# Two attention stages: TensorE issues scores and exponents in pairs and value products two units at a time; VectorE's work between the maxima is put in another order

## What is computed

```python
# first kind, causal (stage a0)
q_rot, k_rot = rotate(q), rotate(k)
scores = einsum('bhqd,bhkd->bhqk', q_rot, k_rot) / sqrt(dh) + decay_bias
scores = where(causal, scores, -inf)
x = x + (softmax(scores) @ v) @ Wo.T
...
# second kind, no mask (stage a1)
q, k, v = layernorm per head of (x @ Wq + bq), (x @ Wk + bk), (x @ Wv + bv)
scores = einsum('bqhd,bkhd->bhqk', q, k) * scale
x = x + (softmax(scores) @ v) @ Wo + bo
```

## Time and profile before

| | |
|---|---|
| median of 3 runs | 2072.04 us (2063.23 to 2077.58) |
| profiled execution | 2082.38 us, its span 2080.5 us |
| TensorE busy | 1543.0 us (74%) |
| VectorE busy | 1178.1 us (57%) |
| ScalarE busy | 720.2 us (35%) |
| GpSimd busy | 940.2 us (45%) |
| `a0` in its steady steps | 410 to 744 us of the span, 11 batches |
| `a1` in its steady steps | 1400 to 1757 us of the span, 10 batches |

### The profile page before, as it was taken

One profiled execution on the slowest core, in us unless ns is written; L12 is line 12 of the kernel. 1 busy time (PEld: TensorE's weight loads), 2 busy tenths in 40 slices (PEclk: granted clock), 3 DMA queues, 4 the chain that ended last, 5 costly groups with the idle time before them and its releaser, 6 DMA issues. The chain is left out here.

```text
span 2080.5 us, 34781 instructions
## 1 busy us (share of the span) xinstructions
PE 1543.0 (74%) x10592; PEld 938.6 (45%) x10592; DVE 1178.1 (57%) x4262; ACT 720.2 (35%) x1339; POOL 940.2 (45%) x1276
## 2 busy tenths in 40 slices
PE   1329938999999998399233992598878788993990
PEld 1219923444444444299222881233333333433880
DVE  3622245566666664122594554777778778843555
ACT  1102213455555553022001330354445445631330
POOL 2745524233443432155474773634454536422771
PEclk9999965999999999599555995587888879965995
DMA  6152210000000000522223882000000000004884
GB/s 219 44 117 66 72 45 16 6 22 16 15 20 10 11 11 13 105 72 69 75 73 97 245 240 67 12 6 16 16 15 14 16 5 11 12 11 106 238 238 130
DMA packets 93868, 134.91 MB, mean 65 GB/s; under 512 B 14784, under 2 KB 72512, under 8 KB 93760
## 3 DMA queue, kind: packets, MB, share of 16 engines
q1 hardware_dynamic: 62768, 88.27, 15.5%
q0 software_dynamic: 17408, 35.82, 5.1%
q10 hardware_dynamic: 13584, 9.48, 1.9%
HBM read 80.61 MB, written 52.91 MB: 64 GB/s over the span
## 5 line engine op out<-in xcount | busy, mean ns | idle before, releaser
L1345 ACT ACTIVATE a_PT<-a_psE 128x512 f32<-128x512 f32 (+1 forms) x512 | 278.0, 543 | 446.0 <-PE a_psE L1509 444.5
L1054 DVE TENSOR_REDUCE a_mx<-a_psS 128x2 f32<-128x512 f32 (+1 forms) x512 | 312.5, 619 | 145.3 <-PE a_psS L1475 144.5
L1532 PE MATMUL a_psV<-a_PT,a_vx 128*32 128x256 f32 (+1 forms) x2048 | 321.8, 397 | 3.0 <-ACT a_PT L1345 0.6
L1475 PE MATMUL a_psS<-a_KT,a_QT 54*128 54x256 bf16 (+1 forms) x1024 | 196.4, 282 | 66.8 <-DVE a_mx L1054 65.5
L1509 PE MATMUL a_psE<-a_QM,a_KT 56*128 56x256 bf16 (+1 forms) x1024 | 199.8, 278 | 1.6 <-issue 0.8
L1907 POOL DMA_INDIRECT slots_y<-e_y,e_ids x160 | 155.3, 970 | 46.6 <-issue 24.4
L1837 PE MATMUL e_psH<-e_rowsT,e_w 128*128 128x256 f32 x640 | 160.3, 395 | 6.4 <-DMA e_w<-in_pack 4.7
L1475 PEld LDWEIGHTS a_psS<-a_KT,a_QT 54*128 54x128 bf16 x1024 | 56.7, 96 | 200.7 <-DVE a_mx L1054 103.5
L1754 POOL DMA_INDIRECT slots_y<-e_y,e_ids x128 | 124.2, 971 | 48.7 <-POOL e_ids L1752 29.2
L1532 PEld LDWEIGHTS a_psV<-a_PT,a_vx 128*32 128x32 f32 x2048 | 77.0, 112 | 118.2 <-issue 82.8
L1837 PEld LDWEIGHTS e_psH<-e_rowsT,e_w 128*128 128x128 f32 x640 | 118.7, 196 | 25.0 <-issue 6.0
(11 more groups left out here) (329 smaller groups left out, 3117.1 us busy)
## 6 DMA issues: line engine op xcount, KB each, us to landing
e_w<-in_pack SPq DMA_DIRECT2D x80, 450.0 KB
e_rows<-slots_x SPq DMA_DIRECT2D x80, 129.0 KB, 2.6
e_rows<-spans_x SPq DMA_DIRECT2D x64, 129.0 KB
a_got<-slots_y SPq DMA_DIRECT2D x32, 256.0 KB
t_got<-slots_y SPq DMA_DIRECT2D x32, 256.0 KB
slots_y<-e_y,e_ids POOLq DMA_INDIRECT x288, 2.2
spans_x<-tail ACTq DMA_DIRECT2D x8, 516.0 KB, 13.4
spans_x<-tail SPq DMA_DIRECT2D x8, 516.0 KB, 17.1
```

The source lines that it names most:

```text
L1054: nc.vector.tensor_reduce(mx[u][:, t, 4 * g + r:4 * g + r + 3:2], psS[c % 2][:, :, 0:cols], AX, ALU.max).then_inc(s_max, 1)
L1345: nc.scalar.activation(PT[:, c % 4, :, q0:SEQ], psE[c % 2][:, :, q0:SEQ], ACT.Exp).then_inc(s_e, 1)
L1475: last = nc.tensor.matmul(psS[c % 2][:, hh, 0:cols], QT[u][64 * r:64 * r + MAXR, k, t * P:(t + 1) * P], KT[u][64 * r:64 * r + MAXR, k, 0:c ...
L1532: last = nc.tensor.matmul(psV[g // 2][32 * quad:32 * quad + 32, g % 2, q0:SEQ], vx[u][:, kt, head, :], PT[:, c % 4, hh, q0:SEQ], start=(kt ...
```

## The change

On TensorE, `unit_scores` and `unit_e` are cut into an opening (waits and, in `a0`, the mask) and single heads. Scores `n+2` and exponents `n+1` are now issued together: both openings, then the heads in turn. `unit_c` gives `r` from `c % 2`, so that the two units of such a pair always lie in different halves of the array. Value products are issued for two units at once, at every even `n`, and the two units now have different `r` and the same tile of keys, so that the four heads lie in four different column strips.

```diff
@@ unit_c @@
-            return c // 4, (c // 2) % 2, c % 2
+            return c // 4, c % 2, (c // 2) % 2
@@ TensorE, step @@
                 if has(s):
-                    unit_scores(s, u, 0)
-                    unit_scores(s, u, 1)
+                    for c in range(2):
+                        scores_open(s, c)
+                    for hh in range(2):
+                        for c in range(2):
+                            scores(u, c, hh)
                 if has(s - 3):
                     routed_tiles(s - 3, v)
+                if has(s - 1):
+                    e_open(s - 1, 0)
+                    for hh in range(2):
+                        e(v, 0, hh)
                 for n in range(UNITS):
-                    if has(s - 1):
-                        unit_e(s - 1, v, n)
-                        if n >= 1:
-                            unit_v(s - 1, v, n - 1)
+
+                    if has(s) and n < UNITS - 2:
+                        scores_open(s, n + 2)
+                    if has(s - 1) and n < UNITS - 1:
+                        e_open(s - 1, n + 1)
+                    for hh in range(2):
+                        if has(s) and n < UNITS - 2:
+                            scores(u, n + 2, hh)
+                        if has(s - 1) and n < UNITS - 1:
+                            e(v, n + 1, hh)
+
+                    if has(s - 1) and n >= 2 and n % 2 == 0:
+                        unit_v(s - 1, v, n - 2)
+                        unit_v(s - 1, v, n - 1)
                     if n == 0 and has(s - 2):
                         back(s - 2, u, 0)
...
-                    if has(s) and n < 14:
-                        unit_scores(s, u, n + 2)
-                if has(s - 1):
-                    unit_v(s - 1, v, 15)
                 if has(s + 1):
                     operands(s + 1, v, 3)
+                if has(s - 1):
+                    unit_v(s - 1, v, UNITS - 2)
+                    unit_v(s - 1, v, UNITS - 1)
```

```diff
@@ Combine @@
+    def dve_add_one(self, dve, link, b, u, w, k, t):
+        link.sync()
+        if k == 0 and t == 0:
+            wait(dve, self.s_got[w], (b - w) * (16 // self.held) + 16)
+        ins = nc.vector.scalar_tensor_tensor(
...
+        if k == TOPK - 1 and t == TPB - 1:
+            link(ins)
+            nc.vector.tensor_copy(self.used[:, u:u + 1], self.gate[:, u, 0:1]).then_inc(self.s_added, 1)
+        else:
+            link.later(ins)
...
@@ VectorE, step @@
-                if has(s - 1):
-                    queries_out(s - 1)
...
                 maxima(0, 1)
-                if has(s + 3) and not causal:
-                    comb.dve_add(dve, link, s + 3, v)
+                if has(s + 3):
+                    comb.dve_gate(dve, link, s + 3, v)
+                add(0, 0)
                 maxima(1, 2)
...
                 if has(s):
                     max_rows(s, u)
+                if has(s + 1):
+                    last_operand_out(s + 1, v)
+                if has(s):
+                    queries_out(s)
+                if has(s - 1):
+                    weighted_out(s - 1, v)
                 if has(s + 3):
                     norm.dve_apply(dve, s + 3, v)
-                if has(s - 1):
-                    weighted_out(s - 1, v)
-                if has(s + 1):
-                    last_operand_out(s + 1, v)
```

89 lines of the change are left out of this document (47 added, 42 removed).

## The result

The changed kernel takes 1991.12 us (median of 4 runs, 1962.49 to 2008.29); the kernel before, beside it on the same chip, 2069.68 us (2063.23 to 2077.58). The ratio is 0.957, with a 95% interval of 0.949 to 0.964. (Disturbed runs are left out of the ratio, which is why it is not the quotient of the medians.) The profiled execution took 1987.22 us with a span of 1985.4. It is faster by 4%; the forecast was 6%.

The account below looks back on a forecast made before the run. TensorE was taken to bound `a0`, waits to decide `a1`. Gains of 88 us in `a0`, 41 in `a1`, 5 at stage ends, less 6 in token stages, took 128 off: profiled 1954, median 1944, range 1888 to 1995.

Parts of the forecast that it names:

- the four strips: TensorE's value products: four heads in four column strips take one unit's time, saving 3.6 us a batch.
- 31.1 at full clock: Batch of `a1`: VectorE's work, gaps and waits at full clock sum to 31.1 us, from 35.7 before.
- hence 32.8: Batch of `a1` with 1.7 us added for TensorE's doubtful clock: 32.8 us, from 30.0 to 35.7.
- Logits, "no wait": VectorE in `a1`: reading the logits later removes their wait, 2.8 us a batch before.
- Projections, "0.9 is left. The second: none": VectorE in `a1`: first projection's wait shrinks to 0.9 us a batch, second's to none; 4.0 us together before.
- The batch's end, 1.4: VectorE waits 1.4 us at each batch's end for operands and queries TensorE transposes last, in `a0` and `a1`.
- Scores met late, 0.9: VectorE in `a1` waits 0.9 us a batch for scores met late.
- The clock, +1.7 for 0.83 and more: TensorE's clock in `a1`, 0.83 before: slow stretches lengthen waits by 0 to 4.5 us a batch, taken as 1.7.
- Additions, "I take VectorE's work as unchanged": VectorE in `a1`: spreading the four additions leaves GpSimd's blocks, so its work stays unchanged.
- The queries first: VectorE's batch end: operand and queries copies directly follow `max_rows`, normalisation and `weighted_out` come behind; 1.4 us of waits.
- Token stages, -6: VectorE in `t1` and `t2`: additions each wait for the one before, losing 4 to 7 us, taken as 6.
- the wait is replaced in `a1`: Rival: low TensorE clock returns the readers' gain at batch's end and projection; `a1` stays 35.7, total 1985 us; 20%.
- The slower rival: Rival: waits at the batch's end make TensorE's clock fall in `a0` too, total 2208 us; 4%.

Follow-up runs that it names:

- kernel 3: Changed kernel with the value products issued one unit at a time behind each pair; 2041.63 us, ratio 0.988 to the kernel before.
- kernel 4: Changed kernel with idle TensorE products in `a1`, 9 before the routed tiles and 8 behind the first pair; 1970.95 us, ratio 0.956.
- kernel 1: Kernel before with only TensorE's new order and the new halves, VectorE's order left old; 2068.4 us, ratio 1.003.
- kernel 11: Changed kernel with the first projection of `a1` one pair later and its reader one maximum later; 2017.5 us, ratio 0.956.
- kernel 9: Changed kernel run again unedited, on another chip; 2033.64 us, ratio 0.962 to the kernel before.
- kernel 10: Changed kernel with idle TensorE products in `a1`, 9 before the routed tiles and 3 behind the first pair; 2023.47 us, ratio 0.956.
- kernel 5: Changed kernel with VectorE's router normalisation behind the next step's first maximum and TensorE's routed tiles later too; 2021.54 us, ratio 0.961.
- kernel 12: Changed kernel with 9 and 3 idle products in `a1` and its first projection one pair later, reader one maximum later; 2000.07 us, ratio 0.946.
- kernel 7: Changed kernel with VectorE's four additions in one block behind the first maximum; 2080.59 us, ratio 0.987.
- Kernel 6: Changed kernel with VectorE's old order at the end of a batch; 2010.71 us, ratio 0.953.
- kernel 2: Kernel before with only VectorE's new order and additions one by one, TensorE's order and halves left old; 2188.68 us, ratio 1.064.
- kernel 8: Changed kernel with VectorE's readers of logits and projections back at their old places, one maximum earlier; 2102.29 us, ratio 0.995.

## Why the prediction was right, and where it was not

**`a0`: TensorE's terms right, the rest partly by luck.** Forecast 24.2 us a batch at full clock, measured 23.8; forecast 88 us, measured 90.1. TensorE's work came to 21.3 us against 21.6. The overlap of the halves, the two masks (0.12 us for the second against 0.11 forecast) and the four strips (0.57 against 0.56) are in the rows above; kernel 3 shows that the strips are worth time. VectorE's sum came out by two errors that cancel: its waits at the batch's end were 0.5 us and not 1.4, those for side results and late scores 2.3 and not 1.8, and its work 20.4 and not 20.2 (388 to 579 us). The sum left out TensorE's wait at line 386, 1.8 us a batch: with it and 0.7 of waits for maxima TensorE fills the batch too. The 88 us are luck in part as well. The clock fell in four late batches (25.1 to 29.3 us), which cost some 15 us (kernel 4, with the same program in `a0`, took 348.5 us for the 15 intervals at full clock, the changed one 364.0); and the first two intervals gave 22.7 us (34.3 and 29.7 before, 19.7 and 21.6 changed) where 5 each were forecast.

**`a1`: the step that failed is the sum of VectorE's waits, "31.1 at full clock" and "hence 32.8"; measured 35.0.** VectorE's work is as forecast, 27.2 us. Its waits for TensorE were put at 3.2 us and 1.7 more for the clock, 4.9 together, and were 7.0:
- *Logits, "no wait"*: 2.6 us. Right.
- *Projections, "0.9 is left. The second: none"*: 2.0 and 1.3 us, 32.1 in ten batches. This is the largest part. I took 2.2 us from the end of maximum 4 to the result; in the rows above it was 5.3 (1495.15 to 1500.48): the logits, which I had left out of this path, took 0.95 (1495.54 to 1496.49), and everything ran at half clock. Kernel 1 shows that the new order of TensorE first makes this wait longer (65.7) and the later reader then takes back that and little more. Kernel 11 shows that it is the place: apart, 5.5 us where kernel 9 had 24.6.
- *The batch's end, 1.4*: 2.4 (17.8 + 5.9 in ten).
- *Scores met late, 0.9*: 1.1, of which the projected output has 1.0 (10.1 in ten) and the prefix sums and scores the rest.
- *The clock, +1.7 for 0.83 and more*: it fell to 0.72, below the 0.75 that I had named as the sign of being wrong. The prediction had TensorE stand still for 3 us behind the first maximum and not for 3.9, and from that took the clock to be no worse. It overlooked the second stop, at line 386: `route.dve_norm` was not among the jobs whose move I followed, although the order of the end of a batch in the changed kernel shows it last. TensorE waits 4.3 us a batch there.

What this stop does to the clock is not shown. Idle products in both of TensorE's stops go with 0.86 (kernel 4) and a shorter wait for the projections; but with the stop at line 386 half filled the clock stays where it was (0.78, kernel 10), without the stop it is 0.68 (kernel 5), and with a longer one 0.87 (kernel 3, where TensorE has more work). Nor is the time that the low clock costs `a1` shown by itself: at 0.86 and 0.87 kernels 4 and 3 still take 34.4 and 35.4 us. What is shown is the projection's place and the idle products together, 34.3 to 32.2 us a batch, the forecast's 32.8 passed: by the profiles 0.8 for the place (kernel 11) and 1.3 for what kernel 12 has beyond it, products and a clock of 0.85.

**Additions, "I take VectorE's work as unchanged".** Right: the work is unchanged, and spreading pays through shorter waits, 3.3 us a batch in `a1` (kernel 7). The prediction used that cover for the logits ("an addition, `split_a`, a maximum and another addition") and, rightly, found no wait left. With the readers' 4.8 us it is what paid for TensorE's new order, which by itself costs `a1` 3.4 us a batch (kernel 1), a cost that stands nowhere in the prediction: it treated TensorE in `a1` as having time to spare.

**The queries first.** I priced the wait and never the gain. Kernel 6 finds no gain to price.

**Token stages, -6.** The copy of the gates and the four additions of a batch in `t2`:

```profile
1950.43 0.17 DVE L234 COPY t_gate_b<-gates 128x4 f32<-128x4 f32 x1
1950.63 1.51 DVE L243 SCALAR_TENSOR_TENSOR x_res<-t_got,t_gate_b,x_res 128x128 f32<-128x128 f32 x4
1952.18 0.15 DVE L251 COPY t_used<-t_gate_b 128x1 f32<-128x1 f32 x1
```

1.51 us against 1.26, and 1.63 in some batches: 0.3 a batch where 0.13 to 0.22 was forecast, 5.0 us in the 16 batches of `t2` and 5.2 in those of `t1`, 10 where 6 were taken. Neither stretch got longer by it: the one from `a0` to `a1` is as long as before and the last one 3.9 us shorter, so something else covers it, presumably the gain in the last step of each attention stage.

**The rivals.** What happened is the second, "the wait is replaced in `a1`", with its 1985 us at 20%: the measured time is nearer to it than to the forecast of 1944, and inside the range. It named the places rightly, the batch's end and the projection; its reason, the low clock, is only in part borne out, as said above. The total is inside the range because the range took this rival in; the forecast's own range, 1925 to 1965, was missed. The rule of the Trainium skill ("TensorE: Matmul & The Clock Gate", section "HAM oscillation — how this bites in real kernels") that idle gaps between bursts of matmuls cost clock named this case. The traces agree in part: in `a0` of kernels 2 and 3 every fall stands behind a stop of TensorE, and with idle products in both stops of `a1` the clock is 0.86; kernels 5 and 10 don't fit a count of stops. The slower rival didn't come in the changed kernel; kernel 2 shows it at work.

**What stays open.** Which of the batches of `a0` lose the clock differs from run to run (none in kernel 4, four late ones in the changed kernel, five of ten in kernel 9, which is the same kernel). On kernel 9's chip even the batches at full clock take 24.6 to 25.1 us and not 23.8, with waits of TensorE for ScalarE that the first profile doesn't have (`a_PT`, 4.3 us in ten batches); why is open. The wait at the batch's end (17.1 us in kernel 12) was left as it is.

## What to carry to other kernels

When one engine's instructions are packed, the readers of that engine's side results have to move with them, and the heaviest side job is better kept out of the packed place: with the readers left where they were the packing was worth nothing here (kernels 1 and 8), and with the projection moved aside another 1.7% came out, with idle products beside it. In a stage where one engine works or waits all the time, add up that engine's waits first: here the other engine's longest wait, 4.3 us a batch, could be taken away without any gain (kernel 5). Follow every job behind a reordered stretch to its reader, the ones that the diff doesn't touch too.

## What the runs showed of the hardware that was not expected

- With a wait of TensorE of 1.1 us in each batch of 31 us (kernel 2, `a0`) the clock fell to half for parts of the batches, to a mean of 0.87, where the kernel before kept 1.00 with 330 of 334 us busy. The changed kernel kept 1.00 from 388 to 579 us with 171 of 191 us busy and a wait of 1.8 us in each batch, and lost it in parts of the batches behind (0.95 over ten). Kernel 3, with the same wait and more work for TensorE (26.5 us busy a batch), had a fall behind each of its ten waits.
- Idle matrix products didn't raise the clock in proportion to the wait that they filled: 17 a batch went with 0.86 (0.72 without, kernel 4), 12 with 0.78 (0.79 without, kernel 10) and, with the projection moved, with 0.85 (0.78 without, kernel 12). Eight of them ahead of products that VectorE needs cost 1.7 us of waits a batch (kernel 4).
- Beside GpSimd: the router's normalisation on VectorE took 2.11 us in `a1` where it takes 0.73 in `a0`, and the copy of the gates 1.24 us in `a1` where it takes 0.17 in `t2`; GpSimd was at work on large tiles in both cases.
